# A four-layer attention kernel: one PSUM bank for the transposes of two attentions, and three general banks

## The chip, the cores and the metric

The kernel runs on one core of a Trainium2 chip, in one launch. The metric is the device time of an execution in microseconds (us); of several executions the median counts. Four compute engines work at once, each through a list of its own in order: TensorE (PE in the rows; its weight loads are PEld), VectorE (DVE), ScalarE (ACT) and GpSimd (POOL). SyncE (SP) starts the transfers. They wait for one another through semaphores. TensorE writes its results to PSUM, which has eight banks of 512 float32 values per partition; ScalarE and VectorE read them from there.

## The reference

Four layers follow one another on `x` and `ctx`, both 8 x 128 x 256 in float32. Cut to what matters:

```python
x = L0(x, ctx)   # 16 heads; mean and deviation of v under the attention's weights, applied to a normalised x
x = L1(ctx, x)   # "second attention": per sequence 128 queries, 256 keys (ctx and x), 16 heads of 16; rmsnorm, MLP
x = L2(x, ctx, ctx)   # two cross attentions, 16 heads of 128, 129 keys; then an MLP of 1024
x = L3(x, ctx)   # "last attention": 16 heads of 16, 128 keys; then an MLP of 1024

def attention_L3(hidden_states, encoder_hidden_states):      # L1 has the same shape of work
    x = layer_norm(hidden_states)
    q, k, v = x @ q_w + q_b, enc @ k_w + k_b, enc @ v_w + v_b  # split in heads
    attn = softmax(q k^T / 4)
    hidden = (attn v) @ cproj_w + cproj_b + hidden_states
    return hidden + gelu(layer_norm(hidden) @ fc_w + fc_b) @ proj_w + proj_b
```

## The kernel before

**Stages.** One after another in time: L0's attention (from 0 to about 199 us), L1's attention (to about 345), L1's MLP (to about 421), the two attentions of L2 (to about 940), L2's MLP (to about 1007), L3's attention (to about 1104, its last units to 1114) and L3's MLP (to the end at 1167).

**Units and ticks.** The attentions of L1 and L3 are cut in units, 64 in L1 and 32 in L3; a unit is one bank of scores. `att_order` writes the order out by hand: at tick u it gives `S` of unit u (scores), `T` of unit u-3 (four transposes of the normalised probabilities, L913), `PV` (probabilities times values, L936) for the units that are ready, and between them the general work that prepares later steps: `pq` and `pk` (selection products, L855 and L862), `dq`, `dk`, `dv` (projections, L768 to L770, twelve matmuls of 256 columns each), `WO` (output projection, also L768 to L770), `nS`, `nX`, `nT` (statistics, scaling and transposes of the next norm) and `w` (splitting of weights). 16 ticks of L1, or 8 of L3, are one iteration and repeat with the same pattern. All engines walk the same order, each doing its own part; VectorE passes it through `late`, which moves the named kinds behind the next `S`.

**What one unit does on each engine.** TensorE writes the scores (L897 in L1, L903 in L3), VectorE takes the maximum (L1619), ScalarE the exponential with its sum (L1274), VectorE the reciprocal (L1570), GpSimd multiplies (L1867), TensorE transposes (L913), then the transposed bank is copied to SBUF: by ScalarE for even units (L1285), by VectorE for odd ones (L1632). The copy of unit u-3 stands in both lists behind the exponential or the maximum of unit u.

**Banks.** Two banks (0, 1) hold scores, two (2, 3) the transposes, two (4, 5) the outputs, and two (6, 7) are general: every piece of general work takes the next of the two in turn (`j_bank`), after the piece before last that used it was read out (`j_full` notes by whom). Before a transpose, TensorE waits for the copy of two units ago:

```python
elif e == "T":
    pe.wait_ge(a["nm"], i + 1)
    if i >= 2:
        copied(pe, ph, i - 2)
```

In L2 the transposes alternate over banks 2 and 3, too; there nothing of this is touched.

**Ends of the attentions.** The last ticks hold the norm that follows: its statistics and its square root (`nS`, L1214, with a load of ScalarE's function table before and after), the scaling of six or four tiles in one go (`nX`, L1508 or L1510), the transposes (`nT`, L802), and the first products of the MLP (`up`, L768 to L770).

**Start.** SyncE sends the rows of biases, the identity and a mask behind the key blocks of step 1 of L0 (L706 to L708). VectorE's `dv` of L0 waits for them (L1806), writes a rounded identity (L1810), and TensorE's first `P2` (L1118) waits for that.

## Time and profile before

| | us |
|---|---|
| three runs | 1166.60, 1164.54, 1166.82 |
| median | 1166.60 |
| the profiled execution, its time | 1168.75 |
| its span in the profile | 1167.0 |
| TensorE busy in the span | 1061.5 (91%) |
| VectorE busy | 728.7 (62%) |
| ScalarE busy | 716.2 (61%) |
| GpSimd busy | 316.8 (27%) |
| chain of work that ended last, TensorE's share | 65% |

The profile gives busy times by engine, the time by stretches, the waits, and each instruction in order of time with the idle time before it and who ended it. The profiled execution took 1168.75 us, 1.75 us of it outside of the span; it is 2.15 us over the median of the three runs.

### The profile page before, as it was taken

What the parts mean: (1) busy time and instruction counts of PE and PEld (TensorE: products, weight loads), DVE (VectorE), ACT (ScalarE), POOL (GpSimd) and SP (SyncE); (2) the same over time, 40 slices, a digit from 0 to 9 for tenths busy, and PEclk for the clock granted to TensorE, in tenths of its full rate; (3) what the DMA queues carried; (4) which work ended last, traced back from release to release, by engine and by line L of the source; (5) the groups of instructions that cost most, each with busy time, mean ns of one, the idle gap of its engine ahead of it and who ended that gap; (6) DMA issues with size and microseconds to landing.
All of it is one profiled execution on the core that took longest, in us unless ns stands there. A gap on an engine that the chain in (4) does not pass through costs nothing.

```text
span 1167.0 us, 24069 instructions
## 1 busy us (share of the span) xinstructions
PE 1061.5 (91%) x8248; PEld 936.3 (80%) x8248; DVE 728.7 (62%) x1755; ACT 716.2 (61%) x2080; POOL 316.8 (27%) x440
## 2 busy tenths in 40 slices
PE   7989897799979999999999979999999989778788
PEld 6767676577759889999998869999998979667588
DVE  6787584677786645555555645555555585767773
ACT  2777765677884465656655556565665552689852
POOL 5242533666540022211111103111111112243311
PEclk8999999899999999999999999999999999999899
DMA  5211111011101021111101001011111110100100
GB/s 169 70 43 46 24 33 42 16 29 25 44 26 46 19 91 46 47 46 47 46 17 71 28 22 45 25 46 46 46 46 37 32 60 1 49 17 19 48 10 28
DMA packets 29853, 48.09 MB, mean 41 GB/s; under 512 B 6627, under 2 KB 20389, under 8 KB 29734
## 3 DMA queue, kind: packets, MB, share of 16 engines
q1 hardware_dynamic: 29638, 46.49, 13.0%
q8 instruction: 68, 1.11, 0.4%
q14 instruction: 51, 0.42, 0.1%
q10 hardware_dynamic: 96, 0.07, 0.0%
HBM read 36.54 MB, written 1.05 MB: 32 GB/s over the span
## 4 chain that ended last, share of the span: by engine, by line
PE 65%; DVE 13%; ACT 10%; issue 7%; POOL 2%; SPq 1%; DMA 1%; ACTq 0%; DVEq 0%; POOLq 0%
PE ps L768 14%; PE ps L769 13%; PE ps L770 13%; PE ps L1012 4%; PE ps L988 4%; PE ps L1150 3%; ACT pt L1274 2%; PE ps L997 2%; DVE nm L1816 2%; PE ps L913 1%; DVE nmax L1619 1%; PE ps L1128 1%; PE ps L1137 1%; PE ps L936 1%; POOL pt L1867 1%
## 5 line engine op out<-in xcount | busy, mean ns | idle before, releaser
L1867 POOL TENSOR_TENSOR pt<-pt,prec 128x256 f32<-128x256 f32 (+1 forms) x224 | 181.3, 810 | 622.9 <-DVE prec L1688 501.1
L1329 ACT ACTIVATE pt<-ps,nmax 128x129 f32<-128x129 f32 x256 | 92.4, 367 | 100.7 <-DVE nmax L1680 99.9
L1475 DVE TENSOR_TENSOR rs<-wraw,rs 128x256 fp32r<-128x256 f32 (+2 forms) x116 | 68.7, 594 | 125.5 <-ACT rs L1205 125.1
L768 PE MATMUL ps<-rs 128*128 128x256 f32 x480 | 142.8, 298 | 4.1 <-DVE rs L1702 2.8
L769 PE MATMUL ps<-rs 128*128 128x256 f32 x480 | 135.9, 283 | 0.0
L770 PE MATMUL ps<-rs 128*128 128x256 f32 x480 | 135.8, 283 | 0.0
L1274 ACT ACTIVATE pt<-ps,nmax 128x256 f32<-128x256 f32 (+1 forms) x256 | 105.3, 425 | 40.3 <-DVE nmax L1619 39.9
L768 PE MATMUL ps<-ht,rs 128*128 128x256 f32 (+1 forms) x304 | 107.5, 354 | 9.0 <-DVE ht L1525 3.0
L770 PE MATMUL ps<-ht,rs 128*128 128x256 f32 (+1 forms) x304 | 100.9, 332 | 0.0
L769 PE MATMUL ps<-ht,rs 128*128 128x256 f32 (+1 forms) x304 | 100.9, 332 | 0.0
L768 PEld LDWEIGHTS ps<-rs 128*128 128x128 f32 x480 | 91.9, 191 | 7.9 <-DVE rs L1702 4.8
L1702 DVE SCALAR_TENSOR_TENSOR rs<-ps,col,rs 128x256 fp32r<-128x256 f32 x128 | 61.9, 483 | 53.4 <-ACT rs L1346 53.4
L769 PEld LDWEIGHTS ps<-rs 128*128 128x128 f32 x480 | 92.0, 192 | 0.0
L770 PEld LDWEIGHTS ps<-rs 128*128 128x128 f32 x480 | 91.9, 191 | 0.0
L768 PE MATMUL ps<-rs,ct 128*128 128x256 f32 x288 | 86.4, 300 | 3.4 <-ACT rs L1256 1.5
L1816 DVE TENSOR_REDUCE nm<-ps 128x2 f32<-128x512 f32 x128 | 82.6, 680 | 6.3 <-PE ps L1128 6.2
L988 PEld LDWEIGHTS ps<-fs 128*128 128x128 f32 x512 | 76.1, 191 | 10.2
L1619 DVE TENSOR_REDUCE nmax<-ps 128x2 f32<-128x512 f32 (+1 forms) x96 | 65.7, 685 | 29.5 <-PE ps L903 24.1
L1369 ACT ACTIVATE fs<-ps,col 128x256 f32<-128x256 f32 x96 | 40.2, 472 | 68.4 <-PE ps L770 67.2
L1417 ACT ACTIVATE pt<-ps 128x512 f32<-128x512 f32 x128 | 73.1, 599 | 13.3 <-PE ps L1137 11.6
L770 PE MATMUL ps<-rs,ct 128*128 128x256 f32 x288 | 80.9, 281 | 0.0
L769 PE MATMUL ps<-rs,ct 128*128 128x256 f32 x288 | 80.9, 281 | 0.0
(206 smaller groups left out, 2999.4 us busy)
## 6 DMA issues: line engine op xcount, KB each, us to landing
wraw<-in_packs SPq DMA_DIRECT2D x52, 512.0 KB, 3.7
rs<-rs SPq DMA_DIRECT2D x222, 32.0 KB, 1.9
bvr<-in_l2rows SPq DMA_DIRECT2D x16, 256.0 KB, 4.5
rs<-rs SPq DMA_DIRECT2D x96, 16.0 KB
row<-in_rows SPq DMA_DIRECT2D x2, 640.0 KB, 4.9
XH<-in_packs SPq DMA_DIRECT2D x2, 512.0 KB, 4.2
out<-X SPq DMA_DIRECT2D x4, 256.0 KB, 2.1
X<-in_x SPq DMA_DIRECT2D x3, 256.0 KB, 3.2
```

What stands on the lines that cost most here:

```text
L768: nc.tensor.matmul(dst, w[0], m[1], start=start, stop=False)
L769: nc.tensor.matmul(dst, w[1], m[0], start=False, stop=False)
L770: return nc.tensor.matmul(dst, w[0], m[0], start=False, stop=stop)
L988: last = nc.tensor.matmul(ps[:, S_BANK + g % 2, b * D:b * D + P + 1], qT[:, hh % 3, 2 * b2 + b, :], kT[:, hh % 3, 2 * b2 + b, :], start=Tr ...
L1274: last = nc.scalar.activation(prob[:, i % PROBS, h * keys:(h + 1) * keys], ps[:, SCORE_BANKS[ph][i % len(SCORE_BANKS[ph])], h * keys:(h + ...
L1329: last = nc.scalar.activation(prob[:, g % PROBS, k * D:k * D + P + 1], ps[:, S_BANK + g % 2, k * D:k * D + P + 1], ACT.Exp, bias=nmax[:, g ...
L1417: nc.scalar.activation(pt[:, i % L0_PTS, :], ps[:, L0_X[i % len(L0_X)], :], ACT.Exp, scale=Q0_SCALE).then_inc(Z["ex"], 1)
L1475: last = nc.vector.tensor_tensor(dst[1], src, f32(dst[0]), ALU.subtract)
L1619: nc.vector.tensor_reduce(nmax[:, i % 4, 0:nh], ps[:, SCORE_BANKS[ph][i % len(SCORE_BANKS[ph])], :].rearrange("p (h n) -> p h n", h=nh), A ...
L1702: nc.vector.scalar_tensor_tensor(cc[1][:, hd, two, :], ps[:, O_BANK + g % 2, 0:D].rearrange("p (b n) -> p b n", b=2), C(f"L2bv{p // PAIRS ...
L1816: nc.vector.tensor_reduce(nm[:, s % 3, im, 2 * p:2 * p + 2], ps[:, L0_S[i % len(L0_S)], :].rearrange("p (h n) -> p h n", h=2), AX.X, ALU.m ...
L1867: nc.gpsimd.tensor_tensor(pr, pr, prec[:, u % 4, 0:nh].unsqueeze(2).broadcast_to([P, nh, keys]), ALU.mult)\
```

## The change

1. **Transposes.** `T_BANKS` is 1 for L1 and L3. All transposes of these attentions go to bank 2, and the transposes of unit i wait for the copy of unit i-1 instead of i-2.
2. **General banks.** Bank 3 joins banks 6 and 7: from L1's first scores to the end of L1's MLP, and from the start of L2's MLP to the end, general work takes the next of three banks. During L2's attentions it is two as before (`rings`, `j_place`, `j_ring`).
3. **ScalarE's order in L3.** `copies_first` puts the copy of unit u-3 ahead of the exponential of unit u.
4. **Norms.** In L1 the scaling is spread over ticks 55, 56 and 57 (all at 55 before). In L3 statistics move from tick 27 to 24, scaling from 28 to 25 and 26, transposes from 30 and 31 to 27 and 29.
5. **Last tail.** In L3 the first three `up` move from ticks 32, 33, 36 to 34, 36, 37.
6. **Start.** The rows and the identity are sent before the key blocks of step 1, and the rounded identity is written before the values of the first sequence.

```diff
@@ att_order
-    first, rest, sqrt = {"L1": (total - 24, total - 4, 10), "L3": (10, total - 3, 5)}[ph]
+    first, rest = {"L1": (total - 24, total - 4), "L3": (10, total - 3)}[ph]
...
-    put(total - sqrt, "nS", after, 0)
-    put(total - sqrt + 1, "nX", after, 0)
-    for n, k in enumerate(GROUPS[after][0]):
-        put(total - sqrt + 3 + (3 if ph == "L1" else 1) * n, "nT", after, k)
+    sums, scale, turn = {"L1": (54, (55, 56, 57), (57, 60, 63)), "L3": (24, (25, 26), (27, 29))}[ph]
+    put(sums, "nS", after, 0)
+    for k in GROUPS[after][0]:
+        put(scale[k], "nX", after, 0, k)
+    for k in GROUPS[after][0]:
+        put(turn[k], "nT", after, k)
     for k in range(2):
-        put(total + k, "up", 0, k)
+        put(total + (k if ph == "L1" else 2 + 2 * k), "up", 0, k)
...
-    put(total + 4, "up", 0, 2)
+    put(total + (4 if ph == "L1" else 5), "up", 0, 2)
...
+def copies_first(order):
+
+    held = []
+    for e in order:
+        if e[0] == "T":
+            yield e
+            yield from held
+            held = []
+        elif e[0] == "S" and T_LAG <= e[1]:
+            held = [e]
+        elif held:
+            held.append(e)
+        else:
+            yield e
+    yield from held
...
@@ build
+        TWO, THREE = (J_BANK, J_BANK + 1), (J_BANK, J_BANK + 1, T_BANK + 1)
+        T_BANKS = {"L1": 1, "L3": 1}
+        rings = {0: TWO}
+
+        def j_place(n):
+
+            since = max(at for at in rings if at <= n)
+            return rings[since][(n - since) % len(rings[since])]
...
-                            if i == 1:
+                            if i == 0:
                                 sp.dma_start(row[:, :, :].rearrange("p r d -> p (r d)"), rows[0].partition_broadcast(P)).then_inc(d_in, 16)
...
@@ TensorE
+            def j_ring(banks, *frees):
+
+                for s, v in freed_by[T_BANK + 1]:
+                    pe.wait_ge(s, v)
+                freed_by[T_BANK + 1] = frees
+                first = j_place(filled[0])
+                rings[filled[0]] = (first,) + tuple(b for b in banks if b != first) if first in banks else banks
...
                 elif e == "T":
                     pe.wait_ge(a["nm"], i + 1)
-                    if i >= 2:
-                        copied(pe, ph, i - 2)
+                    if i >= T_BANKS[ph]:
+                        copied(pe, ph, i - T_BANKS[ph])
...
             for st, *e in first_order():
+                if (st, *e) == ("L1", "S", 0):
+                    j_ring(THREE, (Z["ex"], L0_UNITS))
                 l0(*e) if st == "L0" else att(st, *e)
             for e in mlp_order("L1"):
                 mlp("L1", e)
+            j_ring(TWO)
             wide(wide_order())
+            j_ring(THREE)
@@ ScalarE
-            for e in att_order("L3"):
+            for e in copies_first(att_order("L3")):
                 att("L3", *e)
@@ VectorE
                 elif e == "nX":
...
-                    for b in range(g.start, g.stop):
+                    for b in range(g.start, g.stop) if pair is None else (2 * pair, 2 * pair + 1):
...
+                        nc.vector.tensor_copy(identR, ident[:, :]).then_inc(ident_r, 1)
...
-                    if i == 0:
-                        nc.vector.tensor_copy(identR, ident[:, :]).then_inc(ident_r, 1)
```

The order of TensorE's work does not change within L1's attention; what each row waits for does. Here are ticks 12 and 13 (the transposes of units 9 and 10, a `pq` between them, and scores) before. `L1_teA` and `L1_teD` count the copies that ScalarE and VectorE made, and `L1_nm` the multiplications of GpSimd.

```order
L913 MATMUL ps<-ident,pt 128x128 [waits L1_teD,L1_nm]
L913 MATMUL ps<-ident,pt 128x128 x3
L855 MATMUL ps<-rs,sel 128x256 [waits lat_lo,L1_dense]
L855 MATMUL ps<-rs,sel 128x256 x3
L897 MATMUL ps<-rs 128x512 [waits key_rows_moved1,L1_ex]
L913 MATMUL ps<-ident,pt 128x128 [waits L1_teA,L1_nm]
```

And now:

```order
L949 MATMUL ps<-ident,pt 128x128 [waits L1_teA,L1_nm]
L949 MATMUL ps<-ident,pt 128x128 x3
L891 MATMUL ps<-rs,sel 128x256 [waits L1_dense,L1_hi]
L891 MATMUL ps<-rs,sel 128x256 x3
L933 MATMUL ps<-rs 128x512 [waits key_rows_moved1,L1_ex]
L949 MATMUL ps<-ident,pt 128x128 [waits L1_teD,L1_nm]
```

The transposes of an odd unit (the first row) wait for the other engine than before, since the copy that frees their bank is now that of the unit just ahead, an even one; and the other way round.

ScalarE in a middle tick of L3's attention, before: the work on a `pk` bank and on weights, the four exponentials of a unit (L1274), the copy (L1285), a `dq` or `dk` (L1250).

```order
L1266 CAST rs<-ps 64x2x128 [waits general_bank_filled,L3_sm]
L1205 CAST rs<-wraw 128x256 [waits pack_loaded0]
L1274 ACTIVATE pt,psums<-ps,nmax 128x128 [waits L3_tm,L3_mx]
L1274 ACTIVATE pt,psums<-ps,nmax 128x128 x3
L1285 COPY pt<-ps 128x512 [waits L3_pm,L3_tm]
L1250 ACTIVATE rs<-ps,col 128x256 [waits general_bank_filled]
```

And now:

```order
L1306 CAST rs<-ps 64x2x128 [waits general_bank_filled,L3_sm]
L1245 CAST rs<-wraw 128x256 [waits pack_loaded0]
L1325 COPY pt<-ps 128x512 [waits L3_pm,L3_tm]
L1314 ACTIVATE pt,psums<-ps,nmax 128x128 [waits L3_tm,L3_mx]
L1314 ACTIVATE pt,psums<-ps,nmax 128x128 x3
L1290 ACTIVATE rs<-ps,col 128x256 [waits general_bank_filled]
```

The copy stands ahead of the exponentials of its tick, which no longer hold it up.

TensorE in the last ticks of L3's attention, before: the transposes of units 29 and 30, each followed by a `PV` and by an `up` (twelve matmuls, of which the first and the fourth stand here).

```order
L913 MATMUL ps<-ident,pt 128x128 [waits L3_teD,L3_nm]
...
L936 MATMUL ps<-pt,fs 32x128 [waits L3_teD]
...
L768 MATMUL ps<-ht,rs 128x256 [waits L3nm_lo,L3_done,weight_pack_taken1,weight_pack_taken0]
...
L768 MATMUL ps<-ht,sel 128x256
...
L913 MATMUL ps<-ident,pt 128x128 [waits L3_teA,L3_nm]
...
L936 MATMUL ps<-pt,fs 32x128 [waits L3_teA]
```

And now, for units 29, 30 and 31:

```order
L949 MATMUL ps<-ident,pt 128x128 [waits L3_teA,L3_nm]
...
L972 MATMUL ps<-pt,fs 32x128 [waits L3_teD]
...
L949 MATMUL ps<-ident,pt 128x128 [waits L3_teD,L3_nm]
...
L972 MATMUL ps<-pt,fs 32x128 [waits L3_teA]
...
L949 MATMUL ps<-ident,pt 128x128 [waits L3_teA,L3_nm]
...
L972 MATMUL ps<-pt,fs 32x128 [waits L3_teD]
...
L804 MATMUL ps<-ht,rs 128x256 [waits L3_stA,L3nm_lo,L3_stD,weight_pack_taken1,weight_pack_taken0]
```

The first `up` moved from between the transposes to behind the last of them.

## Rows read from the trace of the kernel before

**Rows 1.** Windows: stretch, its us, busy us of PE, PEld, DVE, ACT, POOL, granted clock.

```profile
241.32:273.95 32.63, 30.87 (x310) 24.89 (x308) 25.11 (x61) 25.99 (x88) 24.67 (x29) 1.00 0.13 26
1055.45:1077.00 21.55, 19.61 (x191) 16.07 (x190) 16.45 (x38) 19.75 (x84) 8.34 (x8) 1.00 0.10 20
222.00:231.00 9.00, 6.91 (x42) 5.28 (x43) 7.41 (x16) 5.37 (x18) 3.70 (x5) 0.63 0.01 2
```

**Rows 2.** Timeline of L1: start, duration, instruction, idle before; units 14 to 16.

```profile
245.31 0.60 PE L913 MATMUL ps<-ident,pt 128*128 128x128 f32 x4
...
247.23 0.66 PE L913 MATMUL ps<-ident,pt 128*128 128x128 f32 x4
247.30 0.61 ACT L1285 COPY pt<-ps 128x512 f32<-128x512 f32 x1
...
248.01 0.67 DVE L1632 COPY pt<-ps 128x512 f32<-128x512 f32 x1
248.05 0.63 PE L913 MATMUL ps<-ident,pt 128*128 128x128 f32 x4
```

**Rows 3.** Timeline of L1, units 18 and 19 with the copy of unit 18.

```profile
252.06 0.60 PE L913 MATMUL ps<-ident,pt 128*128 128x128 f32 x4
...
252.58 0.58 ACT L1291 CAST rs<-ps 128x512 fp32r<-128x512 f32 x1
...
253.19 0.69 DVE L1635 TENSOR_TENSOR rs<-ps,rs 128x512 fp32r<-128x512 f32 x1 [0.91 <-ACT rs L1291]
...
253.80 0.68 DVE L1619 TENSOR_REDUCE nmax<-ps 128x2 f32<-128x512 f32 x1
253.97 0.66 PE L913 MATMUL ps<-ident,pt 128*128 128x128 f32 x4
...
254.51 0.48 ACT L1274 ACTIVATE pt<-ps,nmax 128x256 f32<-128x256 f32 x1 [0.77 <-DVE nmax L1619]
...
255.43 0.58 ACT L1285 COPY pt<-ps 128x512 f32<-128x512 f32 x1
```

**Rows 4.** Timeline of L1: waits of general work for a bank.

```profile
222.70 0.71 PE L862 MATMUL ps<-rs,sel 128*128 128x512 f32 x2 [1.67 <-DVE rs L1581]
...
227.16 1.11 PE L802 MATMUL ps<-ident,X 128*128 128x128 f32 x4 [1.30 <-ACT rs L1266]
...
260.86 0.75 DVE L1581 SCALAR_TENSOR_TENSOR rs<-ps,col,rs 128x512 fp32r<-128x512 f32 x1 [0.97 <-ACT rs L1245]
...
261.76 0.70 PE L862 MATMUL ps<-rs,sel 128*128 128x512 f32 x2 [0.82 <-DVE rs L1581]
```

**Rows 5.** Timeline of L3's first units: waits of general work, and one for keys.

```profile
1016.13 0.46 PE L903 MATMUL ps<-rs 128*128 128x256 f32 x1 [1.36 <-DMA rs<-rs]
1023.65 0.48 PE L862 MATMUL ps<-rs,sel 128*128 128x256 f32 x2 [1.25 <-DVE rs L1588]
1037.72 0.39 PE L768 MATMUL ps<-rs,ct 128*128 128x256 f32 x1 [1.54 <-ACT rs L1256]
```

**Rows 6.** Timeline of L3's last units: waits, and ScalarE's table loads.

```profile
1090.84 1.28 ACT L1214 ACT_TABLE_LOAD   x1
...
1097.01 0.77 PE L903 MATMUL ps<-rs 128*128 128x256 f32 x2 [4.24 <-DVE rs L1616]
1106.60 0.36 PE L768 MATMUL ps<-ht,rs 128*128 128x256 f32 x1 [1.79 <-DVE X L1641]
1113.99 0.42 PE L936 MATMUL ps<-pt,fs 128*32 128x128 f32 x8 [2.31 <-DVE pt L1632]
```

**Rows 7.** Timeline of the start.

```profile
18.68 0.29 SPq L708 DMA_DIRECT2D mraw<-in_mask_s  x1
...
23.66 0.69 PE L1118 MATMUL ps<-rs 128*128 128x128 f32 x2 [2.77 <-DVE rs L1810]
```

**Rows 8.** Timeline of L2's MLP: waits for a bank.

```profile
953.69 0.66 PE L802 MATMUL ps<-ident,XH 128*128 128x128 f32 x4 [1.37 <-ACT fs L1369]
957.23 0.36 PE L768 MATMUL ps<-ht,rs 128*128 128x256 f32 x1 [0.61 <-ACT fs L1369]
```

More of the change, by code:

```diff
@@ L912, in att @@
                     for k in range(4):
-                        last = nc.tensor.transpose(ps[:, T_BANK + i % 2, k * P:(k + 1) * P], prob[:, i % PROBS, k * P:(k + 1) * P],
+                        last = nc.tensor.transpose(ps[:, T_BANK + i % T_BANKS[ph], k * P:(k + 1) * P], prob[:, i % PROBS, k * P:(k + 1) * P],
                                                    ident[:, :])
@@ L1192, in j_take @@
                 act.wait_ge(jm, j + 1)
-                return ps[:, J_BANK + j % 2, :]
+                return ps[:, j_place(j), :]
             def j_skip():
@@ L1284, in att @@
                             act.wait_ge(Z["pm"], L0_STEPS // 2)
-                        nc.scalar.copy(probT[:, i % 3, :], ps[:, T_BANK + i % 2, :]).then_inc(a["teA"], 1)
+                        nc.scalar.copy(probT[:, i % 3, :], ps[:, T_BANK + i % T_BANKS[ph], :]).then_inc(a["teA"], 1)
                 elif e == "OUT":
@@ L1455, in j_take @@
                 dve.wait_ge(jm, j + 1)
-                return ps[:, J_BANK + j % 2, :]
+                return ps[:, j_place(j), :]
             def j_skip():
@@ L1487, in stats, with norm_step @@
                     link(last)
-            def norm_step(e, name, k):
+            def norm_step(e, name, k, pair=None):
                 n = N[name]
-                if e in ("nS", "nX"):
+                if e in ("nS", "nR", "nX"):
                     src = XH if name == "L1r" else X
@@ L1503, in norm_step @@
                 elif e == "nX":
-                    dve.wait_ge(n["sq"], k + 1)
-                    link(nc.vector.reciprocal(sd[:, 3, g], sd[:, 1, g]))
-                    for b in range(g.start, g.stop):
+                    if pair is None or pair == GROUPS[name][k][0]:
+                        dve.wait_ge(n["sq"], k + 1)
+                        link(nc.vector.reciprocal(sd[:, 3, g], sd[:, 1, g]))
+                    for b in range(g.start, g.stop) if pair is None else (2 * pair, 2 * pair + 1):
                         if name == "L1r":
@@ L1575, in att @@
                     mlp(ph, (e, i, *k))
-                elif e in ("nS", "nX", "nT"):
-                    norm_step(e, i, k[0])
+                elif e in ("nS", "nR", "nX", "nT"):
+                    norm_step(e, i, *k)
                 elif e == "dk" and ph == "L1":
@@ L1631, in att @@
                             dve.wait_ge(Z["pm"], L0_STEPS // 2)
[L1632 removed]
+                        nc.vector.tensor_copy(probT[:, i % 3, :], ps[:, T_BANK + i % T_BANKS[ph], :]).then_inc(a["teD"], 1)
                 elif e == "OUT":
```

9 lines of the change are left out of this document (4 added, 5 removed).

## The prediction, made before the changed kernel ran

> **What bounds the kernel now.** I read the windows by stage first. In L1's attention the stretch from the transposes of unit 12 to those of unit 28 is one whole iteration, 32.63 us for 16 units, and TensorE is busy for 30.87 of it at full clock [rows 1]: 95%, so a stall of TensorE there is time of the kernel, with 1.76 us to hide in. In L3's attention an iteration (units 12 to 20) takes 21.55 us, with TensorE busy for 19.61 and ScalarE for 19.75 [rows 1]: both are close to their limit, and neither can win more than about 1.8. Then I read the timeline, looking for two things: where a transpose starts before the copy ahead of it has ended (that is free now and forbidden after the change), and where general work waits for a bank.
>
> **The change part by part, 1: one transpose bank in L1 (a loss).** Two mechanisms put the transposes before the copy of the unit ahead.
>
> The short step. The transposes of unit 15 start at 247.23, VectorE copies them from 248.01 to 248.68, and those of unit 16 start at 248.05 [rows 2], 0.63 ahead of that end. A TensorE instruction that waits starts 0.15 after its releaser's end (261.61 to 261.76) [rows 4]. So with one bank an odd unit and the next are at least 0.78 + 0.67 + 0.15 = 1.60 apart, against 0.82 now. In that iteration the eight steps from odd to even take 1.21, 0.82, 1.21, 2.19, 1.33, 0.73, 1.56 and 0.73 us; the shortfall is 3.4.
>
> The long step. The transposes of unit 18 start at 252.06, but ScalarE copies them only at 255.43, since its list holds an output, a `pq` and the exponential of unit 21 first, which waits for a maximum that stands on VectorE behind the output's low part; the transposes of unit 19 start at 253.97 [rows 3]. The copy ends at 256.01, so with one bank unit 19 would wait 2.04 + 0.15 = 2.19, less what TensorE was held just before. In the same way unit 15 starts 0.68 before the end of copy 14 [rows 2], and unit 21 1.19 before that of copy 20.
>
> The two are not independent: a stall moves the work that drives a later copy, and some of the shortfall is paid by it. Carrying the delay through one iteration, step by step, with a copy shifted by the delay of the scores that drive it, I get for units 14 to 19: 0.38, 0.45, 0.78, 0, 0.38, 1.81 (sum 3.80); units 20 to 22: 0, 1.34, 0.71; then the third general bank gives 0.82 back (the `pk` at 261.76, which waits for a bank only [rows 4]); units 24 to 27: 1.20, 0.82, 0.05, 0, less 0.20 and 0.48 and 0.19 of waits that are overrun; and 0.96 for unit 28, as for unit 12 before. The period grows from 32.63 to about 38.5, by 5.9 us. Its floor is each step taken by itself: odd to even at least 1.60 and even to odd at least 2.13 (a maximum, an exponential and a copy behind the copy ahead) makes 35.5, or 2.8 more. From both sides, then: 2.8 to 5.9 per iteration, and I take the upper, because the long step of rows 3 is there in every iteration with 2.04 us of overlap to lose.
>
> First iteration (units 0 to 11): the same kind of stalls, about 9 us, against waits for a bank of 1.67 and 1.30 [rows 4] and four smaller ones (1.37, 1.31, 0.78, 0.37), 6.8 in all, that the third bank removes: +2.5. Two full iterations: +11.8. Last one up to unit 51: +3.8. The end of L1's attention, where TensorE already idles and the spread scaling takes one lump of 2.5 us from VectorE: 0, from -3 to +3. L1's attention: 2.5 + 11.8 + 3.8 = **+18.1**; by the floors 0 + 5.6 + 2.8 = +8.4.
>
> The PSUM page of the Trainium skill ("PSUM — Partial Sum Buffer", its summary for kernel authors) says that a bank that is being read while TensorE works should not be the one that TensorE writes. The trace can't show the contrary, since the kernel before always writes the other bank; by that rule nothing of the loss can be saved by writing the part of the bank that is copied already.
>
> **2: three general banks elsewhere (a gain).** L2's MLP waits for a bank 1.37 and 0.61 [rows 8]; nothing else is due there: -2.0 (0 to -2.6). The seam into L2 has one such wait of 1.41 on its key evictions, half of it in front of a norm chain that is late anyway: -1 (0 to -1.6). In L3, up to 1016.13 the scores wait for key rows [rows 5], and a bank that comes free sooner only moves the idle time. After it, `pk`, `nT`, `dv` and `dk` wait for a bank for 1.25 and 1.54 [rows 5] and 0.48, 0.28, 0.58 and 0.62, 4.75 in all, while ScalarE idles 4.3 in the same stretch; the one transpose bank costs 1.1 once: -2 (0 to -3.5). L3's middle: bank waits of 0.8 an iteration go, a transpose waits 0.7 behind a late VectorE copy: 0 (from -3 to +2.4 over two iterations).
>
> **3: ScalarE's copy ahead of the exponential in L3.** It makes the transposes of odd units free of waits, and moves even units' exponentials back by 0.35 where ScalarE is busy, or ahead by 0.2 where it waited for a maximum. Part of the 0 above.
>
> **4: the norm in L3's last iteration.** Now the statistics' square root loads a table, 1.28 us [rows 6], and another behind it; with VectorE's four scalings in one go, TensorE waits 4.24 [rows 6]. The loads stay on ScalarE wherever they stand (2.9 with the root), the lump of VectorE is halved and no longer meets the last `WO`: -2.5 (-4.3 to 0).
>
> **5: the last tail.** Two waits, 1.79 and 2.31 [rows 6]: the first `up` waits for its norm, and the last `PV` for a VectorE copy that stood behind two activations' low parts. Both go. In turn three transposes stand close together, 0.85 + 0.75 of new waits, and TensorE's rate should fall to half less often behind them: -3 (-5 to +1).
>
> **6: the start.** TensorE waits 2.77 for the rounded identity, which waits for a transfer issued last at 18.68 [rows 7]. Issued ahead of four key blocks it goes out 3 us sooner; then VectorE, which is at its fourth maximum until 21.06, sets the time: 22.1 instead of 23.66, **-1.6** (-3 to 0). The key blocks of step 1, 1.3 us later, are needed after 22.
>
> **The sum.** 18.1 - 2.0 - 1.0 - 2.0 + 0 - 2.5 - 3.0 - 1.6 = +6.0 us. On the profiled execution: 1168.75 + 6.0 = 1174.7; on the median of the three runs, which is 2.15 lower: 1166.6 + 6.0 = **1172.6 us**. About 0.2%, 2.3 us, is what a measurement of this kernel can tell from no change.
>
> **The rivals.**
> - *Only the floor is lost in L1.* If the copies catch up while TensorE stands still, an iteration loses 2.8, not 5.9, and L1 8.4. Then 1166.6 + 8.4 - 12.1 = 1162.9, faster than before. For it: ScalarE and VectorE are busy for only 26 and 25 of 32.6 us [rows 1]. Against it: in rows 3 ScalarE waits for VectorE and VectorE for ScalarE, and both for scores that come later as well. It decides from a loss of about 14 us in L1 downwards. 0.18, of which a part lies within the bound.
> - *The gains are all there.* Every bank wait of L3 and the seams is won: -12.1 becomes -18 and the time 1166.7. Against it: ScalarE has no more than 1.8 per iteration to give [rows 1]. 0.10.
> - *The clock falls in L1.* From 222 to 231, with waits of 1.67 and 1.30 [rows 4], TensorE had a granted clock of 0.63 of full speed [rows 1], and a block of transposes took 1.11 instead of 0.66: it ran at 1.2 GHz for most of that stretch, behind the first wait. New stalls of 1.8 and 1.3 in each iteration might do the same; a stretch like that one costs 1.5 to 3 us, three of them 4 to 9: 1177 to 1182. 0.17.
> - *The waits don't appear.* The transposes wait but the copies have mostly ended, as the change presumes; then only the gains stay, 1154.5. Rows 2 and 3 speak against it. 0.04.
>
> **How the numbers follow.** The forecast has 0.51, with 1168 to 1178 as its own range. Range for 8 in 10: 1160.5 (the floor case with some of its gains more) to 1181 (the clock case). Faster by over 0.2%: 0.18; within 0.2%: 0.15; slower: 0.67.
>
> **What would show it.** In the changed profile: TensorE's waits at the transposes on VectorE's and ScalarE's copies, some 5 to 8 us per iteration of L1 and absent before; the distance from unit 12 to unit 28 near 38.5; no distance from an odd to the next even unit in L1 under 1.55; the 2.77 at the start down to about 1.2; the waits 4.24, 1.79 and 2.31 down to less than half together; L2's attentions unchanged. An iteration of L1 at 35.5 or less, or L3's attention shorter by over 8 us, would make the prediction wrong.

## The result, and the profile after

| | before | after |
|---|---|---|
| median, us | 1166.7 (4 runs, 1164.5 to 1168.6) | 1184.75 (4 runs, 1183.2 to 1186.9) |
| profiled execution: span, us | 1167.0 | 1185.1 |

The ratio is 1.0159, 95% interval 1.0141 to 1.0176: slower by 18 us. The forecast was 1172.6, 6 us slower; its sign was right, its size a third of what came, and its range (to 1181) does not hold the result.

Each experiment's ratio is to the kernel before as timed beside it (its median lay between 1166.3 and 1167.6 us); small differences between experiments are read from the ratios.

The two traces can be laid over each other by the starts of the 96 blocks of transposes (64 in L1, 32 in L3) and of the MLPs' output additions. The table gives the distance between such marks, us. The first two columns are the kernels before and after; the others are experiments told below (A `e1_l1_two_and_two`, B `e3_l1_one_bank_alone`, C `l1_copy_first`, D `start_alone`, E `copy_first_alone`, F `mix`, G `mix_copy_first`).

| from, to | before | after | A | B | C | D | E | F | G |
|---|---|---|---|---|---|---|---|---|---|
| span's start, L1 unit 0 | 205.0 | 203.6 | 205.9 | 201.1 | 202.8 | 205.1 | 206.3 | 203.1 | 203.0 |
| L1 units 0, 12 | 36.30 | 39.92 | 36.22 | 39.19 | 37.31 | 35.95 | 35.66 | 36.29 | 35.51 |
| 12, 28 | 32.63 | 38.14 | 32.62 | 38.19 | 35.19 | 32.62 | 31.43 | 32.62 | 31.39 |
| 28, 44 | 32.63 | 38.13 | 32.61 | 38.16 | 35.18 | 32.62 | 31.54 | 32.62 | 31.54 |
| 44, 51 | 12.64 | 16.35 | 12.64 | 16.36 | 14.27 | 12.64 | 12.87 | 12.65 | 12.87 |
| 51, 63 | 29.17 | 33.49 | 29.19 | 33.34 | 31.51 | 31.20 | 31.48 | 29.44 | 29.59 |
| 63, first output of L1's MLP | 16.47 | 17.47 | 16.46 | 17.48 | 17.97 | 16.45 | 17.87 | 16.46 | 17.48 |
| first, fourth output | 40.55 | 40.40 | 40.64 | 40.57 | 40.47 | 40.60 | 40.57 | 40.64 | 40.58 |
| to the last scores of L2's attentions | 525.9 | 524.9 | 524.7 | 524.3 | 524.8 | 524.6 | 524.6 | 526.0 | 523.1 |
| to the last output of L2's MLP | 71.25 | 71.19 | 71.22 | 71.23 | 71.22 | 71.25 | 71.24 | 71.22 | 71.23 |
| to L3 unit 0 | 15.72 | 15.71 | 15.58 | 15.99 | 15.39 | 16.21 | 16.13 | 15.97 | 15.36 |
| L3 units 0, 12 | 37.13 | 34.76 | 34.69 | 37.72 | 35.39 | 37.11 | 36.66 | 34.94 | 35.69 |
| 12, 20 | 21.55 | 22.08 | 22.12 | 21.55 | 22.10 | 21.55 | 21.42 | 21.41 | 21.43 |
| 20, 28 | 23.49 | 24.88 | 25.17 | 23.72 | 25.05 | 23.12 | 22.76 | 22.43 | 21.94 |
| 28, second output of L3's MLP | 41.55 | 39.19 | 39.62 | 40.98 | 41.15 | 40.98 | 41.49 | 41.46 | 40.81 |

After against before, the 18.1 us are: to unit 0 -1.5; L1 +3.6, +5.5, +5.5, +3.7, +4.3 and +1.0 behind its last unit (23.7 together); L2 -1.2; L3 -2.4, +0.5, +1.4, -2.4. Where the code is the same on both sides, profiles differ too: up to unit 0 by 7 us, between units 51 and 63 by 2, in L2 by 3. So only the columns together tell what is the change's.

The page of the changed kernel, costliest groups: line, engine, operation, busy us, mean ns of one, idle us just before them and what ended most of it.

```profile
L949 PE MATMUL ps<-ident,pt 128*128 128x128 f32 x384 | 64.5, 294 | 52.0 <-DVE pt L1673 30.6
```

TensorE idles 52.0 us in front of the transposes, 30.6 of it for VectorE's copies. Before the change the same group had 2.0, and none of it for a copy:

```profile
L913 PE MATMUL ps<-ident,pt 128*128 128x128 f32 x384 | 62.6, 288 | 2.0 <-POOL pt L1867 1.6
```

TensorE's idle time as a whole rose by only 17.7 us, from 105.5 to 123.2: much of what it now waits here, it waited elsewhere before. The windows that answer to [rows 1] (first iteration from L1's first scores, units 12 to 28, 51 to 63; L3's units 12 to 20 and 20 to 28; columns as there):

```profile
198.24:243.47 45.23, 33.23 (x247) 26.50 (x246) 29.14 (x69) 29.32 (x86) 25.59 (x24) 0.85 0.09 19
243.47:281.61 38.14, 30.82 (x309) 24.65 (x309) 25.50 (x61) 26.59 (x85) 24.68 (x28) 1.00 0.11 22
336.09:369.58 33.49, 23.31 (x208) 18.70 (x209) 23.91 (x55) 23.73 (x66) 12.29 (x11) 0.85 0.08 23
1074.03:1096.11 22.08, 19.44 (x190) 15.91 (x189) 16.19 (x38) 19.53 (x84) 8.32 (x8) 1.00 0.09 19
1096.11:1120.99 24.88, 17.44 (x167) 13.18 (x166) 18.90 (x48) 22.84 (x86) 8.32 (x8) 1.00 0.13 35
```

In L1's iteration TensorE does the same 30.8 us of work at the same full clock, and 5.5 us of idle time are added: no slower work, only waits.

The timeline of L1 that answers to [rows 2, 3]: units 14 to 16 and 18, 19.

```profile
247.86 0.63 PE L949 MATMUL ps<-ident,pt 128*128 128x128 f32 x4 [0.22 <-DVE pt L1673]
...
249.47 0.60 ACT L1325 COPY pt<-ps 128x512 f32<-128x512 f32 x1
...
250.22 0.63 PE L949 MATMUL ps<-ident,pt 128*128 128x128 f32 x4 [0.33 <-ACT pt L1325]
...
250.88 0.69 DVE L1673 COPY pt<-ps 128x512 f32<-128x512 f32 x1 [0.21 <-PE ps L949]
...
251.72 0.63 PE L949 MATMUL ps<-ident,pt 128*128 128x128 f32 x4 [0.65 <-DVE pt L1673]
...
258.19 0.47 ACT L1314 ACTIVATE pt<-ps,nmax 128x256 f32<-128x256 f32 x1 [0.76 <-DVE nmax L1660]
...
259.10 0.58 ACT L1325 COPY pt<-ps 128x512 f32<-128x512 f32 x1
...
259.83 0.63 PE L949 MATMUL ps<-ident,pt 128*128 128x128 f32 x4 [1.69 <-ACT pt L1325]
```

In the short step unit 16 starts 1.50 behind unit 15 (0.66 to the copy, 0.69, 0.15), where it stood 0.82 behind. In the long step unit 19 waits 1.69 for a copy that stands on ScalarE behind an exponential that itself waited for a maximum.

L1's end, the place that the forecast put at 0. ScalarE and TensorE around unit 52:

```profile
337.35 1.28 ACT L1254 ACT_TABLE_LOAD   x1
340.65 0.30 ACT L1254 ACTIVATE sd<-sd,eps 128x6 f32<-128x6 f32 x1 [2.02 <-DVE sd L1540]
340.97 1.28 ACT L1314 ACT_TABLE_LOAD   x1
...
343.18 0.58 ACT L1325 COPY pt<-ps 128x512 f32<-128x512 f32 x1
343.91 1.09 PE L949 MATMUL ps<-ident,pt 128*128 128x128 f32 x4 [4.28 <-ACT pt L1325]
```

The root of the norm waits 2.02 for its statistics (0.33 before the change) with ScalarE's queue behind it, then a table is loaded and two exponentials come, and only then the copy of unit 52: 5 us after its transposes began. Unit 53 waits 4.28 for it. Behind that wait the transposes take 1.09 us in place of 0.60, and the granted clock is 0.50 from 343 to 349. Before the change unit 53 did not wait for that copy; it started 3.61 ahead of the copy's end:

```profile
323.77 0.66 PE L913 MATMUL ps<-ident,pt 128*128 128x128 f32 x4
...
326.80 0.58 ACT L1285 COPY pt<-ps 128x512 f32<-128x512 f32 x1
```

L2's MLP, which answers to [rows 8]:

```profile
972.48 1.28 ACT L1409 ACT_TABLE_LOAD   x1
973.77 1.57 ACT L1409 ACTIVATE fs<-ps,col 128x256 f32<-128x256 f32 x4
...
974.76 0.36 PE L804 MATMUL ps<-ht,rs 128*128 128x256 f32 x1 [1.03 <-ACT fs L1409]
...
980.60 0.36 PE L804 MATMUL ps<-rs 128*128 128x256 f32 x1 [0.87 <-issue]
```

The transposes no longer wait 1.37, but the product behind them waits 1.03 for the same activation, and 0.87 comes up later. A third wait, 0.71 before for VectorE's low part of an activation, is 1.17 now. The table load and the activation on ScalarE stand where they stood.

L3's last iteration, which answers to [rows 6]: VectorE ahead of the copy of unit 27, then the transposes of unit 28.

```profile
1117.82 1.36 DVE L1515 TENSOR_TENSOR sel<-wraw,sel 128x512 fp32r<-128x512 f32 x1 [0.31 <-ACT sel L1245]
1119.10 0.41 DVE L1565 CAST ht<-XH 128x512 fp32r<-128x512 f32 x1
1119.55 0.69 DVE L1566 TENSOR_TENSOR ht<-XH,ht 128x512 fp32r<-128x512 f32 x1
1120.16 0.68 DVE L1673 COPY pt<-ps 128x512 f32<-128x512 f32 x1
...
1120.99 1.09 PE L949 MATMUL ps<-ident,pt 128*128 128x128 f32 x4 [3.07 <-DVE pt L1673]
```

The norm's low parts (L1565, L1566), which the change moved here, and a weight's stand ahead of the copy that alone frees the bank. TensorE also waits 0.99, 1.17, 1.63, 1.46 and 0.41 at transposes in this iteration.

The start, which answers to [rows 7]: the first P2, and the scores of a later step.

```profile
20.92 0.41 PE L1154 MATMUL ps<-rs 128*128 128x128 f32 x2 [0.28 <-POOL rs L1977]
...
27.85 0.50 PE L1164 MATMUL ps<-rs 128*128 128x512 f32 x1 [2.32 <-DMA rs<-rs]
```

The 2.77 went down to 0.28: the first P2 came at 20.92, 2.74 us sooner. Then 0.67 and 2.32 came up behind it for key rows, whose transfers had been moved back, and the fifth P2 came only 0.43 sooner (40.24 for 40.67).

### The profile page after: what moved, and what is told of

The parts are those of the page before. It is cut to its first block, busy times and chain, and to the rows that moved or that the text cites. A ratio compares the mean times of both kernels' runs of the same rounds, so it can differ in the third digit from the quotient of the medians.

```text
span 1185.1 us, 24067 instructions
## 1 busy us (share of the span) xinstructions
PE 1061.9 (90%) x8248; PEld 938.4 (79%) x8248; DVE 730.5 (62%) x1755; ACT 717.2 (61%) x2080; POOL 316.9 (27%) x440
## 4 chain that ended last, share of the span: by engine, by line
PE 64%; DVE 15%; ACT 10%; issue 8%; POOL 1%; SPq 1%; DMA 1%; DVEq 0%; ACTq 0%; POOLq 0%
PE ps L804 14%; PE ps L805 14%; PE ps L806 14%; PE ps L1048 4%; PE ps L1024 4%; PE ps L949 3%; PE ps L1186 3%; ACT pt L1314 2%; PE ps L1033 2%; DVE nm L1856 2%; DVE pt L1673 2%; DVE nmax L1660 1%; PE ps L1164 1%; PE ps L1173 1%; ACT pt L1325 1%
## 5 line engine op out<-in xcount | busy, mean ns | idle before, releaser
L949 PE MATMUL ps<-ident,pt 128*128 128x128 f32 x384 | 64.5, 294 | 52.0 <-DVE pt L1673 30.6
L949 PEld LDWEIGHTS ps<-ident,pt 128*128 128x128 f32 x384 | 44.6, 148 | 69.7 <-issue 42.1
L804 PE MATMUL ps<-rs,ct 128*128 128x256 f32 x288 | 86.6, 301 | 0.6 <-DVE fs L1705 0.4
```

Source lines behind the costliest of these rows:

```text
L804: nc.tensor.matmul(dst, w[0], m[1], start=start, stop=False)
L949: last = nc.tensor.transpose(ps[:, T_BANK + i % T_BANKS[ph], k * P:(k + 1) * P], prob[:, i % PROBS, k * P:(k + 1) * P], ident[:, :])
```

## The experiments

All were compared with the kernel before on the same chip. Diffs are against the changed kernel unless said otherwise.

**1. `e1_l1_two_and_two`: two and two banks in L1 again.**

```diff
-        T_BANKS = {"L1": 1, "L3": 1}
+        T_BANKS = {"L1": 2, "L3": 1}
...
-                if (st, *e) == ("L1", "S", 0):
-                    j_ring(THREE, (Z["ex"], L0_UNITS))
```

> The changed kernel, with L1's attention put back to two banks for transposes and two general ones; all else stays. Theory A: the one transpose bank makes all of L1's loss, its last units included, since ScalarE's copy of unit 52 stands behind the square root of the norm and unit 53 now waits 4.28 us for it. Then the distance from unit 12 to unit 28 is 32.6 again, from unit 51 to unit 63 29.2 (now 33.5), and the time is 1184.8 - 22.8 = about 1162 us (1160.5 to 1163.5). Rival B: only the 17.5 us up to unit 51 come from the bank, and the 4.3 behind it from the scaling that is spread over three units; then unit 51 to 63 stays near 33 and the time is about 1167.

Measured: 1164.3 us, ratio 0.9979 (0.9965 to 0.9993). Column A: every distance of L1 is that of before within 0.1 us, from unit 51 to 63 too. So the bank makes the whole loss, the 4.3 at the end included (theory A), and the rest of the change gives about 2.4 us. That is less than theory A reckoned: the time lies 0.8 above its range. The 1.0 us behind unit 63 is less certain than the 4.3: experiments 4 and 9, with one bank in L1, took 16.46 there, as before the change.

**2. `e2_l1_scaling_in_one`: L1's scalings not spread.**

```diff
-    sums, scale, turn = {"L1": (54, (55, 56, 57), (57, 60, 63)), "L3": (24, (25, 26), (27, 29))}[ph]
+    sums, scale, turn = {"L1": (54, (55, 55, 55), (57, 60, 63)), "L3": (24, (25, 26), (27, 29))}[ph]
```

> The changed kernel, with L1's norm scaled in one go behind unit 52's exponentials, as before the change (unit 55 for all three pairs in place of 55, 56, 57). Theory A (the one bank makes the loss at the end of L1's attention): the time stays 1184.8, within 1.5 us, and the distance from unit 51 to unit 63 stays 33.5, within 1.5. Rival B (the spread scaling makes it): that distance falls by 3 to 5 us and the time to 1180 to 1182.

Measured: 1183.0, ratio 1.0154 (1.0127 to 1.0181). Units 51 to 63 took 31.79, 1.7 less. But five profiles with this part as in the changed kernel gave 33.49, 33.37, 33.68, 33.30 and 32.04, and the 32.04 is the one in which the granted clock was 0.95, as here; the others had 0.80 to 0.85. Most of the 1.7 goes with the clock; the spreading costs at most a fraction of it. Experiment 3 says the same: it has one bank and the norm in one go as before the change, and takes 33.34 at a clock of 0.85.

**3. `e3_l1_one_bank_alone`: one transpose bank in L1 and no third general one.** Against the kernel before:

```diff
-                    if i >= 2:
-                        copied(pe, ph, i - 2)
+                    if i >= (1 if ph == "L1" else 2):
+                        copied(pe, ph, i - (1 if ph == "L1" else 2))
```

and `T_BANK + i % (1 if ph == "L1" else 2)` in the three places that name the bank.

> The kernel before, with one edit: L1's transposes use one bank, and the other one is left empty, so that the general work has two banks as ever. If the third general bank is worth in L1 what the prediction took (6.8 us in the first iteration, 0.8 in each later one), L1 loses 22.8 + 9 = 32 us and the time is about 1198. If waits for a general bank are absorbed by the waits for a copy (the rival), it loses about 22.8 and the time is 1189 to 1191.

Measured: 1188.0, ratio 1.0188 (1.0168 to 1.0209). This is the rival, a little under its 1189. An iteration takes 38.19 and 38.16 with two general banks, 38.14 and 38.13 with three; the first twelve units 39.19, against 38.6 to 40.8. The third bank, to which the prediction gave 6.8 us in the first iteration and 0.82 in each later one, gives L1 nothing there, and 0.82 ahead of unit 0 (first scores to unit 0: 6.12 here, 5.31 in the changed kernel). While TensorE stands at a transpose, the general work's bank comes free anyway: from L1's first scores to unit 12 the bank waits of 6.8 us are down to 3.1 here, without a third bank, and to 0.8 with it, for the same loss (2.9 and 2.8).

**4. `e4_l3_two_and_two`: two and two banks in L3 alone.**

```diff
-        T_BANKS = {"L1": 1, "L3": 1}
+        T_BANKS = {"L1": 1, "L3": 2}
...
+            j_ring(TWO)
             for e in att_order("L3"):
```

> The changed kernel, with L3's attention put back to two banks for transposes and two general ones; its new norm, last units and ScalarE's copy ahead of the exponentials stay. Theory C: the moved norm and the new last units would give their 4 to 5 us, but the one bank takes it again in waits of 1.16, 1.62, 3.07 and 1.46 at the transposes of units 24, 26, 28 and 30. Then units 20 to 31 take 28 to 29 us in place of 32.6, the first twelve units lose the 2.4 that the third bank gave, the middle wins 0.5 per iteration, and the time is 1181 to 1183. Rival D: the moves give nothing in themselves; units 20 to 31 stay at 32 to 33, and the time is 1186 to 1187.

Measured: 1187.3, ratio 1.0186 (1.0166 to 1.0206). Units 0 to 12 lost 1.9 (36.65), units 12 to 20 won 0.65 (21.43), 20 to 28 won 1.7 (23.14), and 28 to the second output lost 2.5 (41.65). From unit 20 to 31 it took 31.0 (expected 28 to 29, before 33.5), but the MLP behind came no sooner: from unit 20 to its second output 64.8, against 64.1 and 65.0 in the changed kernel and before. Neither theory has it all: units 20 to 31 come between the two, but the time is near rival D's. With two banks the moved norm and products give nothing to the end either.

**5. `l3_ups_back`: the three `up` products of L3's end in their old places.**

```diff
-        put(total + (k if ph == "L1" else 2 + 2 * k), "up", 0, k)
+        put(total + k, "up", 0, k)
...
-    put(total + (4 if ph == "L1" else 5), "up", 0, 2)
+    put(total + 4, "up", 0, 2)
```

> The changed kernel with one edit: in L3's last units the three up products stand at ticks 32, 33 and 36 again, where they stood before the change, and not at 34, 36 and 37; the norm stays where the change put it. In the changed kernel the last WO addition comes 39.7 us behind the transposes of unit 20 (before 42.0), but the second MLP output 24.4 behind that addition (before 23.0). Theory E: the up products were done in TensorE's waits and are now left for the tail. Then the second figure falls to 22 to 23, the first stays under 40.5, and the time is 1.5 to 2.5 us less, 1182.3 to 1183.3. Rival F: an up product ahead of the last transposes holds the last copies up by as much as it takes out of the tail; the time stays within 1 us of 1184.8 or rises.

Measured: 1185.1, ratio 1.0148 (1.0132 to 1.0165). From the last WO addition to the second output 22.2 in place of 24.4, as theory E says; but the addition itself came 42.7 behind unit 20, not 39.7. The sum, 64.9, is no less than the changed kernel's 64.1 or the 64.8 to 66.2 of four other profiles with the same L3 (A, C, experiments 2 and 7): rival F. The products can be done in the attention's waits or in its tail, and cost the same.

**6. `l1_copy_first`: ScalarE's copy ahead of its tick's exponentials in L1 too.**

```diff
-            for st, *e in first_order():
+            for st, *e in copies_first(first_order(), ("L1",)):
```

(ScalarE's loop only; `copies_first` looks behind the stage's name.)

> The changed kernel with one edit: in L1's attention too ScalarE's copy of transposes stands ahead of the exponentials (and of the other work) of its tick. It tells how much of L1's loss is the long step, in which ScalarE copies late. In the changed kernel TensorE waits in an iteration 3.6 us at transposes for ScalarE's copies and 3.7 for VectorE's, and 4.28 once for copy 52. If the long step is a cost of its own (theory G), the 3.6 go down to under 1.5, the distance from unit 12 to unit 28 falls from 38.1 to 35.5 to 36.5, and the time by 6 to 10 us to about 1177. If the exponentials that come later cost as much as the copy wins (rival H), the distance stays 37.5 or more and the time at 1183 or more.

Measured: 1172.5, ratio 1.0052 (1.0035 to 1.0070): 12 us less than the changed kernel, and more than theory G's 6 to 10. Its window from unit 12 to 28, and its transposes of units 18 and 19 with the copy between:

```profile
240.15:275.34 35.19, 30.88 (x309) 24.65 (x309) 24.98 (x61) 26.71 (x85) 24.73 (x28) 1.00 0.12 24
```

```profile
252.47 0.63 PE L950 MATMUL ps<-ident,pt 128*128 128x128 f32 x4 [0.22 <-DVE pt L1674]
...
253.66 0.60 ACT L1326 COPY pt<-ps 128x512 f32<-128x512 f32 x1
...
254.42 0.66 PE L950 MATMUL ps<-ident,pt 128*128 128x128 f32 x4
```

Copy 18 now begins 0.56 behind the end of its transposes, not 2.36, and unit 19 does not wait. No transpose of the iteration waits for ScalarE; those that wait 4.2 us wait for VectorE. So 2.95 of the iteration's 5.5 us go with the place of ScalarE's copy, and 2.55 are left. This does not price the long and the short step by themselves: with two banks the same edit takes 1.2 us off an iteration (experiments 12 and 13). In that order of ScalarE's work one bank costs 35.19 against 31.4, 3.8 us; in the old one it costs 5.5.

**7. `root_later`: L1's statistics and root at unit 55, behind copy 52.**

```diff
-    sums, scale, turn = {"L1": (54, (55, 56, 57), (57, 60, 63)), "L3": (24, (25, 26), (27, 29))}[ph]
+    sums, scale, turn = {"L1": (55, (56, 57, 57), (57, 60, 63)), "L3": (24, (25, 26), (27, 29))}[ph]
```

> The changed kernel with one edit: in the last units of L1's attention the norm's statistics and square root stand at unit 55 in place of 54 (the scalings at 56, 57, 57 in place of 55, 56, 57). At 54 the root, which waits 2.02 us for the statistics and loads a table, stands on ScalarE ahead of its copy of unit 52, and the transposes of unit 53 wait 4.28 for that copy. At 55 it stands behind that copy and ahead of a copy that VectorE makes. Theory K: this wait made the unforeseen loss at the end of L1's attention. Then it falls under 1.5, the distance from unit 51 to unit 63 falls from 33.5 to 31 to 32, and the time by about 2 us to 1182.5 to 1183.5. Rival L: the root's wait and its loads stand in ScalarE's way wherever they are; the distance stays over 33.

Measured: 1185.0, ratio 1.0147 (1.0127 to 1.0167). The wait of unit 53 fell to 2.44, and unit 53 came 1.8 sooner; ten units later 0.5 was left (32.95). The root no longer waits for its statistics. But copy 52 now stands behind an exponential that waits 3.10 for its maximum, and copy 54 behind the root and its loads; units 55 and 56 wait 0.99 and 2.96, where unit 56 alone waited 2.04:

```profile
336.01 0.47 ACT L1314 ACTIVATE pt<-ps,nmax 128x256 f32<-128x256 f32 x1 [3.10 <-DVE nmax L1660]
...
336.93 0.58 ACT L1325 COPY pt<-ps 128x512 f32<-128x512 f32 x1
337.53 1.28 ACT L1254 ACT_TABLE_LOAD   x1
```

Rival L in the main, at nearly the number it gave: the loads stand in the way at either place.

**8. `l3_exp_first`: the copy behind the exponentials in L3, as before the change.** (`for e in att_order("L3")` in ScalarE's loop.)

> The changed kernel with one edit: in L3's attention ScalarE's copy stands behind the exponentials of its tick again, as before the change, while the transposes keep their one bank. If the place of the copy costs in L3 what it costs in L1, where 12 us went with it, the distance from unit 12 to unit 20 grows from 22.1 to 23.5 to 25 and the time by 3 to 7 us. The prediction took this edit's worth in L3's middle as part of a sum of 0; the rival is that ScalarE, busy for 19.5 of 22.1 us, sets the time in either order, and that the distance stays within 0.4 of 22.1.

Measured: 1190.4, ratio 1.0203 (1.0179 to 1.0227). The interval lies above the changed kernel's (1.0141 to 1.0176): about 5 us slower. Units 12 to 20 take 22.10, against 22.08: in the middle the rival holds, that the order makes no difference there. The 3 to 7 us of the other theory came all the same, but elsewhere. By the profiles L3 is longer by 1.8, 0.9 of it in units 0 to 12. The profile is of the fastest of four executions (1186.4, the others 1188.4 to 1192.5), so it does not show where the rest went.

**9. `l3_no_root`: L3's first norm without its root, so without two table loads.**

```diff
-                    nc.scalar.activation(sd[:, 1, g], sd[:, 0, g], ACT.Sqrt,
+                    nc.scalar.activation(sd[:, 1, g], sd[:, 0, g], ACT.Identity if (name, k) == ("L3nm", 0) else ACT.Sqrt,
```

> The changed kernel without the square root of L3's first MLP norm: the variances pass through ScalarE as they are, so that neither the table for the root nor the one for the exponentials behind it is loaded (1.28 us each); part of the computation is left out. In the last iteration of L3's attention, from the transposes of unit 20 on, ScalarE is busy for 25.1 of the 27.9 us to its last exponential. Theory M: this stretch is bound by ScalarE, so moving the root within it gives nothing, and taking the two loads out gives nearly all of 2.6: from unit 20 to unit 28 22.3 to 23 us in place of 24.9 to 25.2, to the second MLP output 61.5 to 62.5 in place of 64.1 to 64.9, and the time about 2.3 less, 1182.5. Rival N: TensorE's waits on its one bank set the end; the loads come out of ScalarE's idle time and the time falls by less than 1.

Measured: 1185.9, ratio 1.0157 (1.0138 to 1.0175). Its window of units 20 to 28:

```profile
1098.52:1121.91 23.39, 17.15 (x168) 13.09 (x166) 18.96 (x48) 20.30 (x84) 8.32 (x8) 0.99 0.14 37
```

ScalarE has 2.54 less to do, the stretch is 1.5 to 1.8 shorter, and unit 20 to the second output takes 63.0 in place of 64.1 to 64.9. (The windows of the changed kernel give 24.7 busy us of ScalarE in the 27.9, not 25.1.) The time did not fall; 1.1 to 1.9 us are within what its four executions scatter. By the profiles the truth is between M and N: of the 2.54 some 40 to 75% came off the stretch. What holds the rest is not shown by this run alone; unit 28 waits 3.07 in this kernel too, for a copy behind the same work of VectorE.

**10. `start_alone`: the start's part alone.** Against the kernel before: `if i == 0` for `if i == 1` at the identity's transfer, and its rounding ahead of the first value biases.

> The kernel before with one part of the change: the identity's transfer goes out ahead of four key blocks and VectorE rounds it ahead of the first value biases. The first P2 then comes at 20.5 to 21.7 us in place of 23.7, but the scores of the third step, behind it, wait 1.5 to 2.3 us for the rows whose transfers were moved back. Theory I: 0.5 to 1.5 us of the 2.7 are left, the time is about 1165.3 and the fifth P2 comes 0.5 to 2 us sooner. Rival J: nothing is left; 1166.3 and the fifth P2 at 40.7.

Measured: 1166.4, ratio 0.9993 (0.9979 to 1.0007). The first P2 came at 21.91, the fifth at 39.72 (before 23.66, 40.67); three waits for key rows, 0.63, 0.86 and 1.91, went with it, and about half of the 1.75 was left. That speaks for theory I, but the time alone does not tell it from nothing.

**11. `mix`: what wins, put together.** L1 at two and two, L3 at one and three up to unit 12 and at two and two behind it, the `up` products in place.

```diff
+        PAIRED = {"L1": 0, "L3": 12}
+        def t_bank(ph, i):
+            return T_BANK + (i % 2 if i >= PAIRED[ph] else 0)
...
+                if e == ("T", PAIRED["L3"] + 1):
+                    j_ring(TWO)
```

> A mixed version, to see whether the parts that win add up: the changed kernel with L1's attention at two transpose banks and two general ones (as in the first experiment, 1164.3 us), L3's attention at one and three only up to unit 12, where it won 2.4 us, and at two and two behind it, where one bank costs 0.55 per iteration, and the three up products of L3 in their places of before. By theory: 1164.3 - 0.55 - 0.5 - 2 = 1161 to 1162. If the end of L3 is bound by ScalarE however TensorE's waits lie (rival), only the middle is won: 1163.5.

Measured: 1164.0, ratio 0.9977 (0.9965 to 0.9990). Column F: L3 up to unit 12 34.94, 12 to 20 21.41, 20 to 28 22.43, all as hoped for, and 28 to the second output 41.46, no shorter. The time is the rival's (1163.5), 2 us over the theory's. The gain over the first experiment is not measurable, though L3 by itself is 1.4 us shorter.

**12. `mix_copy_first`: the same, with the sixth experiment's edit.**

> The mixed version (ratio to before 0.9977) with ScalarE's copy ahead of the exponentials in L1's attention too. With one transpose bank that took 12 us off. Here L1 has two transpose banks, an iteration of 32.6 us with TensorE busy for 30.9 of it, so that no more than 1.7 an iteration can be won. Theory G says that the copy's place costs only where a transpose waits for it: with two banks it does not, and the distance from unit 12 to 28 stays 32.6 within 0.5, the time within 1 us of the mixed version's. Rival: the later exponentials hold the scores up, and the iteration grows by 1 or more.

Measured: 1158.4, ratio 0.9931 (0.9911 to 0.9952), the fastest of all. Theory G missed, and so did its rival: the iteration is shorter. Its windows from unit 12 to 28 and from 51 to 63:

```profile
238.55:269.94 31.39, 30.52 (x309) 24.96 (x308) 25.05 (x61) 26.27 (x87) 24.68 (x29) 1.00 0.13 27
314.35:343.94 29.59, 20.43 (x213) 15.70 (x209) 26.34 (x60) 24.65 (x71) 13.56 (x12) 1.00 0.10 26
```

The iteration is 1.23 shorter. TensorE's idle time in it fell from 1.76 [rows 1] to 0.87 and its busy time from 30.87 to 30.52. Not all of the 5.7 us between the profiles of this kernel and of `mix` is this edit's: 2.9 are L1 from unit 0 to 51, and 2.9 lie in L2's attentions, where the code is the same.

**13. `copy_first_alone`: only that edit, on the kernel before.**

> The kernel before with one edit: ScalarE's copy of transposes stands ahead of the exponentials of its tick in both attentions; banks, norms, last units and start as before the change. In the mixed version this edit shortened L1's attention up to unit 51 by 2.9 us, against the theory that the copy's place costs only with one bank. If that is the edit's own (theory G2: a TensorE wait for the copy two units back, or for the PV behind it, goes), L1 up to unit 51 takes 111.3 in place of 114.2 us, and the time is 1163 to 1164.5. If it came with the mixed version's other parts, L1 stays 114.2 within 0.5 and the time 1166 to 1167.5.

Measured: 1167.1, ratio 0.9996 (0.9986 to 1.0006). The same two windows:

```profile
241.92:273.35 31.43, 30.58 (x310) 25.01 (x309) 25.07 (x61) 26.31 (x87) 24.64 (x29) 1.00 0.14 27
317.76:349.24 31.48, 23.04 (x212) 18.13 (x209) 25.94 (x60) 24.63 (x71) 13.39 (x12) 0.89 0.09 24
```

L1 from unit 0 to 51 takes 111.5 as G2 says, so the 2.7 us are the edit's own. But the waits that G2 names are little of it: in an iteration no transpose waited for a copy before, and the `PV` waits went from 0.20 to 0.08. The waits at scores fell from 0.48 to 0.18 and one at a `pk` from 0.82 to 0.59. And the time did not fall, where G2 gave 1163 to 1164.5. In the profile the 2.7 us are gone by the MLP: units 51 to 63 took 2.3 more than before, at a granted clock of 0.89, and TensorE's same work is 23.04 busy us there against 20.43 in `mix_copy_first` at 1.00; another 1.4 is lost behind unit 63 (17.87 at 0.90, against 16.47 at 1.00). Why `mix_copy_first` keeps the clock more often (the mean granted clock of its runs is 0.981 to 0.990, here 0.976 to 0.981) was not settled.

## Why the prediction was wrong

| step | foretold | measured | by |
|---|---|---|---|
| L1, first iteration | +2.5 | +2.8 from the first scores | windows |
| two full iterations | +11.8 | +11.0 | table |
| last one, to unit 51 | +3.8 | +3.7 | table |
| end of L1's attention | 0 (-3 to +3) | +5.3 (4.3 to unit 63, 1.0 behind it) | table, experiment 1 |
| L2's MLP | -2.0 | -0.1 | table |
| seam into L2 | -1.0 | 0 | table |
| L3's first units | -2.0 | -2.4 | table, experiments 3, 4 |
| L3's middle | 0 | +0.5 | table, 4, 8 |
| norm and last tail | -5.5 | -1.0, and 0 within the scatter | 4, 5, 9, 11 |
| start | -1.6 | -0.7 at the first scores | windows, 10 |

With the 1.2 us of scatter in L2 the measured column makes 18 us. The 12 that the sum was short of are 5.3 at L1's end, 4.5 at L3's, 1.9 in L2's MLP and 0.9 at the start, less 0.6 in the rest of L1.

- **The two mechanisms in L1 were right, and their size nearly**: 38.14 for a foretold 38.5, and wait by wait (1.69 at unit 19 for 1.81, 0.65 at unit 16 for 0.78, 0.70 at unit 22 for 0.71). But added up as printed the terms of the working make 7.2 us, not 5.9; the waits at transposes came to 7.3 and the iteration grew by 5.5. That the foretold 5.9 lies so near has luck in it. The floor, too, comes out higher from the rows: the shortfall of the odd-to-even steps is 3.6, not 3.4, and with both floors the iteration is 36.7, not 35.5. That experiment 6 measured 35.19 does not confirm the floor, as its edit shortens the iteration with two banks too.
- **The third bank gave L1's iterations nothing.** In the first iteration both amounts came: waits at transposes rose from 1.7 to 10.7 us, the 9 that were charged, and the bank waits of 6.8 fell to 0.8. But without a third bank they fall to 3.1 and the loss is the same (experiment 3). The sum of +2.5 was nearly right, its reason was not.
- **The step that failed most is "the end of L1's attention ... 0"** (5.3 of the 12 us, of which the bank is shown to make the 4.3 up to unit 63). The reason given was that TensorE idles there already. But before the change it idled elsewhere than at the transposes: unit 53 started 3.61 ahead of the end of copy 52, the largest overlap of all L1, behind the root and a table load. The hand calculation stopped at unit 51, one unit ahead of it. The sentence on the clock held in its mechanism: the waits came, and the clock with them fell, here and not in the iterations (1.00). From unit 51 to 63 one bank costs 2.6 us at equal clock (31.8 and 32.0 at 0.95, against 29.2 and 29.4 at 0.94) and the profiles at 0.80 to 0.85 are another 1.5 longer.
- **"Both go" was true of the waits and false of the time** in L3's end (4.5 of the 12 us). The waits of [rows 6] are gone, and those at transposes (0.99, 1.17, 1.63, 3.07, 1.46, 0.41; 8.7 us) took their place. Even with two banks (experiment 4) nothing was won. Two parts of the reason are shown: ScalarE's work, the two loads included, which the move took along, is in part what sets the stretch (experiment 9), and an `up` not done in a wait is done behind it (experiment 5). From unit 20 to the second output the profiles with L3 as changed took 64.1 to 66.2, those with L3 as before 64.1 to 65.0. The prediction read the waits of one engine, and counted the work only at the place from which it was moved.
- **L2's MLP** (1.9 of the 12): the waits for a bank were waits for ScalarE's activation, read through the bank it frees. With another bank TensorE waits for the activation itself, 1.03, and for VectorE's part behind it, 1.17.
- **The seam**: the changed kernel's L2 is 1.2 us shorter, but so are those of experiments 3, 10 and 13, which have the old seam. It is scatter.
- **The start**: what is late next was named (the key blocks of step 1 "are needed after 22") and not priced; in the changed kernel's profile it took 2.3 of the first P2's 2.7 us by the fifth P2, with the start alone about half. Nor did VectorE's fourth maximum hold the first P2 to 22.1; it came at 20.92.
- Of the tells, the distance of unit 28, the 5 to 8 us of waits an iteration (7.3), the start's wait (0.28, for about 1.2), the waits 4.24, 1.79 and 2.31, and L2's attentions came out; "no odd to even step under 1.55" did not quite, with 1.50, as the copy follows its transposes sooner, 0.66 for 0.78.
- The rule of the Trainium skill ("PSUM — Partial Sum Buffer", its summary for kernel authors), to write another bank than the one being read, was kept by every kernel and so not put to a test: each writes its transposes only after the copy of what lay in the bank.

## What to carry to other kernels

Before a buffer is made single, list for every use how far its next writer runs ahead of its last reader, the exceptional places (norms, table loads, the end of a loop) as well as the steady ones; each overlap is a wait to come, and a smaller one where the reader can be moved to the front of its queue. A wait for a bank is the wait for the engine that frees it, so a further bank helps only where TensorE's next work needs nothing else from that engine. In a stretch that a second engine nearly fills, stalls taken off the first give back no more than the second one's idle time, so read both before adding up.

## What the runs showed that was not expected

- A copy ahead of the exponentials shortens L1's iteration even with two transpose banks: 32.62 to 31.4 us (experiments 12 and 13).
- TensorE's granted clock at L1's end differs from run to run of like code: units 51 to 63 took 29.17 at 0.94 (before) and 31.20 at 0.84 (experiment 10) with the same code, 29.19 at 1.00 with the scaling spread (experiment 1), and the stretch behind unit 63 took 16.45 to 16.47 at 1.00 in six profiles of fifteen and 17.46 to 17.97 at 0.90 in the other nine. A gain of 2.7 us just ahead of it disappeared there (experiment 13).
- A switch of ScalarE's table shows its 1.28 us and no more in the rows at L1's end: the exponential at 342.27 begins 0.02 behind the end of the load at 340.97. Two loads taken out made 2.54 us of ScalarE's busy time (experiment 9).
